# Layer 0 feed-forward: the normalisation and the first scaling of a tile of x move from VectorE to ScalarE, and the measuring of the rows moves within VectorE's tile

## The chip, the cores and the metric

The kernel is one program on one core of a Trainium2 chip. The engines have these names: PE is TensorE (matmuls and transposes, PEld its weight loads), DVE is VectorE, ACT is ScalarE, POOL is GpSimd, and SP issues transfers. The time is device microseconds of the program, from its start to its end; the median of several runs is what is compared. All times in the text are microseconds (us) unless marked ns.

## The reference, cut to what matters

The program computes four layers on x, which is 16 tiles of 128 rows by 256 columns in float32. Each layer is an attention-like part and a feed-forward part, each added to x. The change is in the feed-forward part of layer 0, which works on quantised numbers (a "BitNet" linear layer with a Hadamard transform):

```
x = x + _L0_ffn_ref(_layernorm(x), w_gate, w_up, w_down)

def act_quant(x):                       # per row
    scale = 128 / clip(max(|x|), 1e-5)
    return clip(round(x * scale), -128, 127) / scale
def weight_quant(w):                    # -1, 0, 1 times a mean
    ...
def fwht(x):                            # Walsh-Hadamard transform over 1024 columns
    ...
gate = act_quant(x) @ weight_quant(w_gate).T        # 256 -> 1024
up   = act_quant(x) @ weight_quant(w_up).T          # 256 -> 1024
return act_quant(fwht(silu(gate) * up)) @ weight_quant(w_down).T   # 1024 -> 256
```

`_layernorm` subtracts the row's mean and divides by the root of its variance plus 1e-5.

## The kernel before, in words

The stage is the function `hadamard_ffn`. It handles the 16 tiles t = 0 to 15 as a pipeline written out by hand: each engine has its own program, a function `tile(t, u)` called for every t (u is t modulo 2, the buffer), and the engines meet only at semaphores. An engine does its instructions strictly in the order written; a wait holds everything behind it. `over_long_pipe` calls `tile` for t = 0 and 1, then in a loop for t = 2 to 11, then for the last four written out. `ahead(t, n)` says that tile t + n exists.

What happens to one tile, by engine:

- VectorE, `quantise_x` (L221, then L1348 to L1362): `normalise` writes `xn`, from which the largest magnitude of each row is reduced into `a_max`; `a_rec` is its reciprocal and `deq` the factors for gate and up; then L1358 multiplies `xn` by `a_rec` and adds the constant MAGIC (which rounds), and L1362 subtracts MAGIC again and clips at 127 into the bf16 tile `xq`. Each step is followed by a `drain`, since the next reads what it wrote.
- TensorE, `turn_xq`: two transposes of `xq` into PSUM. ScalarE, `copy_xqT`: copies them to SBUF. TensorE, `gate_up`: eight matmuls of 128x512 in bf16. ScalarE, `silu` (L1428): the gate. VectorE, `gate_times_up` (L1369): gate times up into `prod`.
- GpSimd, `butterflies` (L1336, L1337): six additions and subtractions of 128x512 in float32, between tiles in SBUF, from `prod` by way of `fly` to `mixed`. These are three of the transform's levels. TensorE, `turn_mixed`: eight transposes in two halves, each half copied by ScalarE's `copy_mixedT` (L1434). TensorE, `transform`: 16 matmuls with the Hadamard matrix into `ps_f`.
- VectorE, `scale_h` (L1374 to L1380): largest magnitude of each row of `ps_f`, its reciprocal `b_rec`. ScalarE, `round_h` (L1440). VectorE, `quantise_h` (L1386). TensorE `turn_hq`, ScalarE `copy_hqT`, TensorE `down` (into `ps_y`). VectorE, `add_to_x` (L1390): adds `ps_y` to x, and takes the row statistics for the next stage.

In one call of `tile(t)`, VectorE does quantise_x(t+3), gate_times_up(t+2), scale_h(t), add_to_x(t-1), quantise_h(t). ScalarE does copy_mixedT(t) twice, silu(t+2), copy_hqT(t-1) twice, copy_xqT(t+3), round_h(t). TensorE does turn_mixed(t, first half), the gate of t+2, turn_mixed(t, second half), the up of t+2, transform(t) with turn_hq(t-1) between its halves, turn_xq(t+3), down(t-1). `down(t-1)` also waits for copy_xqT(t+3), since both use the PSUM tile `ps_q`.

Ahead of the first tile GpSimd computes the power -0.5 of all 16 tiles' variances in one instruction (L216, `all_rstd`), then fills a tile of zeros and the one-column tile `magic`. ScalarE waits for `magic` (`const_done`).

Of the kernel before, what the change touches and what calls it, by code (L numbers as in the profile page):

```python
# [8 lines left out]
P = 128  # L9
# [49 lines left out]
        body(t, t % 2)  # L59


def over_ring(eng, body, n, ring, lead=1):

    rest = n % ring or ring
    for j in range(lead * ring):
        body(j, j % ring)
    with eng.Fori(lead, (n - rest) // ring) as i:
        for r in range(ring):
            body(i * ring + r, r)
    for j in range(n - rest, n):  # L70
        body(j, j % ring)
# [1194 lines left out]
def hadamard_ffn(core, name):  # L1266
# [3 lines left out]
    with core.stage() as st:  # L1270
# [3 lines left out]
        def sem(n):  # L1274
            return core.sem(f"{name}_{n}", st)
# [44 lines left out]

        @block.gpsimd
        def _(pool):
            all_rstd(pool, core, rstd_done)
            pool.memset(core.zeros[:, :], 0.0).then_inc(zeroed, 1)
            pool.memset(magic[:, :], MAGIC).then_inc(const_done, 1)

            def butterflies(t, u):

                pool.wait_ge(prod_done, t + 1)
                if after(t, 2):  # L1330
                    pool.wait_ge(mixT_put, t - 1)
                for n, (src, dst) in enumerate(((prod[u], fly), (fly, prod[u]), (prod[u], mixed[u]))):
                    v, o = (m[:, :].rearrange("p (a two c) -> p a two c", two=2, c=P << n) for m in (src, dst))
                    if n:
                        pool.drain()
                    pool.tensor_tensor(o[:, :, 0, :], v[:, :, 0, :], v[:, :, 1, :], ALU.add)  # L1336
                    last = pool.tensor_tensor(o[:, :, 1, :], v[:, :, 0, :], v[:, :, 1, :], ALU.subtract)  # L1337
                last.then_inc(mixed_done, 1)

            over_tiles(pool, butterflies)  # L1340

        @block.vector
        def _(dve):
# [61 lines left out]
            dve.wait_ge(rstd_done, 1)
            quantise_x(0, 0)
            quantise_x(1, 1)
            gate_times_up(0, 0)
            quantise_x(2, 0)
            gate_times_up(1, 1)  # L1410
            over_long_pipe(dve, tile)
            add_to_x(B - 1, 1)
            finish_stats(dve, core)

        @block.scalar
        def _(act):
# [32 lines left out]
            def tile(t, u):  # L1449
# [19 lines left out]
            copy_hqT(B - 1, 1)

# [1314 lines left out]
```

## Time and profile before

| what | us |
|---|---|
| median of 3 runs | 1633.55 (1631.49 to 1633.68) |
| the profiled execution's own time | 1628.51 |
| its span | 1626.7 |
| VectorE busy over the whole span | 1071.2 (66%) |
| TensorE busy | 1352.0 (83%) |
| ScalarE busy | 777.4 (48%) |
| GpSimd busy | 631.9 (39%) |

The stage of the change lies between about 273 us (the last row statistics of the stage before are done) and 456 us in the trace. Busy shares over the whole span say little about it, since the eight stages have different limits; it is read by itself, in the timelines below. Matmuls overlap, so their busy times are not exact, and the names of buffers are without their numbers.

### The profile page before, as it was taken

How to read it: one execution, taken by the hardware profiler on the slowest of the kernel's cores; microseconds unless marked ns; L12 is line 12 of the kernel's file. 1: busy time of each engine (PE TensorE's matmuls, PEld its weight loads, DVE VectorE, ACT ScalarE, POOL GpSimd, SP SyncE). 2: the span in 40 equal slices, each digit the busy share in tenths (PEclk: the TensorE clock that was granted, in tenths of full speed). 3: DMA queues.
4: the chain of work that ended last, by engine and by line, in shares of the span. 5: the costliest groups of instructions: out<-in, count | busy, mean ns of one | idle time of the engine just before them, and what ended most of it. 6: DMA issues, size and time to landing. Idle time of an engine off the chain costs nothing. (4 is left out here: it accounts for less than half of the span.)

```text
span 1626.7 us, 29297 instructions
## 1 busy us (share of the span) xinstructions
PE 1352.0 (83%) x7976; PEld 845.5 (52%) x7992; DVE 1071.2 (66%) x2429; ACT 777.4 (48%) x2322; POOL 631.9 (39%) x649
## 2 busy tenths in 40 slices
PE   3899996566759969799997999978995999978993
PEld 2555553345534434476554666554663666654662
DVE  3898896788748855422664888875334888864224
ACT  2676773344540025432105888842442788833330
POOL 3112420777757523474002112112444665214661
PEclk9999997899979959999997999998998999998997
DMA  4231001400010022397501000141442210411224
GB/s 151 76 83 48 17 15 62 149 0 0 1 52 0 0 84 75 109 303 222 157 1 48 25 28 22 49 159 43 133 128 74 65 49 29 172 55 56 84 84 162
DMA packets 96447, 124.80 MB, mean 77 GB/s; under 512 B 11117, under 2 KB 76464, under 8 KB 96112
## 3 DMA queue, kind: packets, MB, share of 16 engines
q1 hardware_dynamic: 85392, 95.63, 18.5%
q0 software_dynamic: 10608, 28.07, 5.9%
q8 instruction: 36, 0.59, 0.1%
q14 instruction: 43, 0.35, 0.1%
q10 hardware_dynamic: 368, 0.16, 0.0%
HBM read 91.31 MB, written 33.43 MB: 77 GB/s over the span
## 5 line engine op out<-in xcount | busy, mean ns | idle before, releaser
L695 ACT ACTIVATE l0a_prob<-l0a_ps_s,l0a_neg_max 128x128 f32<-128x128 f32 x512 | 137.6, 398 | 67.7 <-DVE l0a_neg_max L553 60.0
L695 ACT ACTIVATE l2a_prob<-l2a_ps_s,l2a_neg_max 128x128 f32<-128x128 f32 x512 | 138.3, 399 | 26.7 <-DVE l2a_neg_max L553 21.7
L1135 ACT ACTIVATE l3a_prob<-l3a_ps_s,l3a_neg_max 128x256 f32<-128x256 f32 x256 | 104.3, 482 | 33.9 <-DVE l3a_neg_max L1050 32.3
L216 POOL TENSOR_TENSOR ln_rstd<-ln_var_eps,minus_half 128x16 f32<-128x16 f32 x7 | 20.5, 2922 | 233.5 <-POOLq L171 207.0
L553 DVE TENSOR_REDUCE l2a_neg_max<-l2a_ps_s 128x4 f32<-128x512 f32 x128 | 85.5, 683 | 19.1 <-PE l2a_ps_s L793 18.1
L501 POOL TENSOR_TENSOR l2a_k_head<-l2a_kT,head_of_row 128x512 f32<-128x512 f32 x32 | 32.9, 1047 | 161.7 <-DMA l2a_kT<-k_rows 161.7
L562 DVE COPY l0a_probT<-l0a_ps_t 128x512 f32<-128x512 f32 x128 | 84.4, 680 | 15.4 <-PE l0a_ps_t L805 15.2
L1050 DVE TENSOR_REDUCE l3a_neg_max<-l3a_ps_s 128x2 f32<-128x512 f32 x128 | 84.0, 679 | 14.2 <-PE l3a_ps_s L1186 13.0
L553 DVE TENSOR_REDUCE l0a_neg_max<-l0a_ps_s 128x4 f32<-128x512 f32 x128 | 85.2, 681 | 10.4 <-PE l0a_ps_s L793 9.6
L1748 PE MATMUL l1a_ps_y<-l1a_kv,l1a_tap 128*128 128x512 f32 x192 | 84.3, 602 | 3.7 <-POOL l1a_kv L1720 3.7
L501 POOL TENSOR_TENSOR l0a_k_head<-l0a_kT,head_of_row 128x512 f32<-128x512 f32 x30 | 30.8, 1047 | 145.6 <-DMA l0a_kT<-k_rows 145.6
L805 PE MATMUL l2a_ps_t<-ident,l2a_prob 128*128 128x128 f32 x512 | 75.6, 281 | 8.0 <-DVE l2a_probT L562 7.0
L805 PEld LDWEIGHTS l2a_ps_t<-ident,l2a_prob 128*128 128x128 f32 x512 | 56.7, 142 | 42.5 <-DVE l2a_probT L562 24.7
L2607 PE MATMUL l3f_ps_g<-l3f_w_gu_all,l3f_xinT 128*128 x156 | 73.5, 593 | 0.0
L805 PE MATMUL l0a_ps_t<-ident,l0a_prob 128*128 128x128 f32 x512 | 69.9, 273 | 1.8 <-DVE l0a_probT L562 1.8
L1198 PE MATMUL l3a_ps_t<-ident,l3a_prob 128*128 128x128 f32 x512 | 69.1, 278 | 2.2 <-ACT l3a_probT L1143 2.0
L1720 POOL TENSOR_TENSOR l1a_kv<-l1a_vT,ctxT_all 128x1024 f32 (+1 forms) x32 | 61.6, 1947 | 18.8 <-PE l1a_ps_y L1748 18.5
L2297 DVE TENSOR_TENSOR l3f_h_sb<-l3f_ps_g,l3f_act_sb 128x256 f32<-128x256 f32 x39 | 16.5, 424 | 77.9 <-ACT l3f_act_sb L2453 77.9
L562 DVE COPY l2a_probT<-l2a_ps_t 128x512 f32<-128x512 f32 x96 | 64.6, 681 | 4.4 <-PE l2a_ps_t L805 4.4
L783 PE MATMUL l0a_ps_s<-l0a_mask,identb 128*128 128x512 bf16 x128 | 49.7, 397 | 21.0 <-ACT l0a_prob L695 21.0
L2071 POOL DMA_INDIRECT l2f_xin<-expert_rows,l2f_tokens x47 | 44.6, 949 | 55.4 <-PE l2f_ps_x L2593 42.1
L1198 PEld LDWEIGHTS l3a_ps_t<-ident,l3a_prob 128*128 128x128 f32 x512 | 56.9, 142 | 17.1 <-ACT l3a_probT L1143 10.9
(477 smaller groups left out, 3532.4 us busy)
## 6 DMA issues: line engine op xcount, KB each, us to landing
l1f_w_gu<-in_l1f_w_gu SPq DMA_DIRECT2D x32, 352.0 KB, 6.8
expert_results<-zeros SPq DMA_DIRECT2D x1, 8320.0 KB, 26.3
l1f_got<-expert_results SPq DMA_DIRECT2D x16, 512.0 KB, 3.9
expert_results<-l2f_y_sb SPq DMA_DIRECT2D x47, 128.0 KB, 1.7
l1f_w_d<-in_l1f_w_d SPq DMA_DIRECT2D x32, 176.0 KB
l2f_w_gu_all<-in_l2f_w_gu SPq DMA_DIRECT2D x1, 4096.0 KB, 15.2
l3f_w_gu_all<-in_l3f_w_gu SPq DMA_DIRECT2D x1, 4096.0 KB, 15.4
l3f_got<-expert_results SPq DMA_DIRECT2D x16, 256.0 KB, 5.0
```

Of the source, the lines that this page charges most:

```text
L501: pool.tensor_tensor(k_head[u][:, c, :, :], kT[u][:, c:c + 1, :].broadcast_to([P, R, P]), core.head_of_row[:, :].unsqueeze(2).broadcast_to ...
L553: dve.tensor_reduce(neg_max[:, j, :], ps_s[j][:, :].rearrange("p (r k) -> p r k", r=R), AX.X, ALU.max, negate=True).then_inc(max_done, 1)
L562: dve.tensor_copy(probT[4 * c + j][:, :], ps_t[j % 2][:, :]).then_inc(t_done_v, 1)
L695: last = act.activation(prob[4 * c + j][:, r * P:r * P + P], ps_s[j][:, r * P:r * P + P], ACT.Exp, bias=neg_max[:, j, r:r + 1])
L783: pe.matmul(ps_s[j][:, :].rearrange("p (r k) -> p r k", r=R), core.identb[:, :], mask[u][:, :].unsqueeze(1).broadcast_to([P, R, P]), start ...
L805: last = pe.transpose(ps_t[j % 2][:, r * P:r * P + P], prob[4 * c + j][:, r * P:r * P + P], core.ident[:, :])
L1050: dve.tensor_reduce(neg_max[:, j, :], ps_s[j][:, :].rearrange("p (r k) -> p r k", r=2), AX.X, ALU.max, negate=True).then_inc(max_done, 1)
L1135: last = act.activation(prob[4 * c + j][:, m * D:m * D + D], ps_s[j][:, m * D:m * D + D], ACT.Exp, bias=neg_max[:, j, m:m + 1])
L1198: last = pe.transpose(ps_t[j % 2][:, k * D + m * P:k * D + m * P + P], prob[4 * c + j][:, m * D + k * P:m * D + k * P + P], core.ident[:, :])
L1720: pool.tensor_tensor(kv[u][:, c, :].rearrange("p (b j i) -> p b j i", b=B, i=N8), i_rows, j_rows, ALU.mult).then_inc(kv_done, 1)
L1748: last = pe.matmul(ps[u][c][:, cols], tap[u][:, (c - m) * P:(c - m) * P + P], kv[u][:, m, cols], start=(m == 0), stop=(m == c))
L2607: last = pe.matmul(ps_g[r % 2][:, 0:2 * FE], xinT[r % 2][:, c, :], w, start=(c == 0), stop=(c == KC - 1))
```

## The change

Five things change, all in `hadamard_ffn`:

1. The normalisation is done by ScalarE (`norm`) as rstd times x plus `shift`, where `shift` = -mean times rstd is one small VectorE instruction for tiles 0 to 2 and one for 3 to 15. `xn` has two buffers. It is done for tile t+5 at the end of ScalarE's tile t.
2. The multiplication by `a_rec` with the addition of MAGIC is done by ScalarE (`round_x`) into a new tile `xr`, for tile t+4, behind `round_h(t)` and ahead of `norm(t+5)`.
3. VectorE's `quantise_x` becomes `measure_x` (reduction, scale, reciprocal, `deq`) for tile t+4 and `clip_x` (the clipping into `xq`) for tile t+3. Both now stand behind `scale_h(t)` and ahead of `add_to_x(t-1)`; before, the whole stood first in the tile.
4. The power is taken in two parts, of 3 and of 13 columns, each with its own signal.
5. The loop now covers t = 2 to 9, and the last six tiles are written out.

TensorE's program is the same as before, and so are GpSimd's six butterflies per tile.

The core of the diff:

```diff
+def rstd_in_parts(pool, core, done):
+    for part in (slice(0, FIRST), slice(FIRST, B)):
+        pool.tensor_tensor(core.rstd[:, part], core.var_eps[:, part], core.minus_half[:, part], ALU.pow).then_inc(done, 1)
...
-            def quantise_x(t, u):
-                dve.drain()
-                normalise(dve, core, xn[:, :], t)
-                dve.drain()
-                dve.tensor_reduce(a_max[:, :], xn[:, :], AX.X, ALU.max, apply_absolute_value=True)
...
-                dve.tensor_scalar(xn[:, :], xn[:, :], a_rec[:, :], MAGIC, ALU.mult, ALU.add)
-                dve.drain()
+            def measure_x(t, u):
+                dve.wait_ge(normed, t + 1)
+                dve.tensor_reduce(a_max[u][:, :], xn[u][:, :], AX.X, ALU.max, apply_absolute_value=True)
+                dve.drain()
+                dve.tensor_scalar(a_max[u][:, :], a_max[u][:, :], 1e-5, 1.0 / 128, ALU.max, ALU.mult)
+                dve.drain()
+                dve.reciprocal(a_rec[:, :], a_max[u][:, :]).then_inc(x_scaled, 1)
+                dve.tensor_scalar(deq[u][:, :], w_mean[:, 0:2], a_max[u][:, :], None, ALU.mult)\
                    .then_inc(deq_done, 1)
+            def clip_x(t):
+                dve.wait_ge(x_rounded, t + 1)
                 if after(t, 1):
                     dve.wait_ge(xqT_put, t)
+                dve.tensor_scalar(xq[:, :], xr[:, :], MAGIC, 127.0, ALU.subtract, ALU.min).then_inc(xq_done, 1)
...
             def tile(t, u):                      # VectorE
-                if ahead(t, 3):
-                    quantise_x(t + 3, 1 - u)
                 if ahead(t, 2):
                     gate_times_up(t + 2, u)
                 scale_h(t, u)
+                if ahead(t, 3):
+                    clip_x(t + 3)
+                if ahead(t, 4):
+                    measure_x(t + 4, u)
                 if after(t, 1):
                     add_to_x(t - 1, 1 - u)
                 quantise_h(t)
...
+            def norm(t, u):                      # ScalarE
+                act.activation(xn[u][:, :], core.xt(t), ACT.Identity, bias=shift[:, bass.ds(t, 1)],
+                               scale=core.rstd[:, bass.ds(t, 1)]).then_inc(normed, 1)
+            def round_x(t, u):
+                act.wait_ge(x_scaled, t + 1)
+                if after(t, 1):
+                    act.wait_ge(xq_done, t)
+                act.activation(xr[:, :], xn[u][:, :], ACT.Identity, bias=magic[:, :], scale=a_rec[:, :])\
+                    .then_inc(x_rounded, 1)
...
                 if ahead(t, 3):
                     copy_xqT(t + 3, 1 - u)
                 round_h(t)
+                if ahead(t, 4):
+                    round_x(t + 4, u)
+                if ahead(t, 5):
+                    norm(t + 5, 1 - u)
```

Ahead of the loop, ScalarE now does norm(0), norm(1), the wait for `magic`, round_x(0), round_x(1), copy_xqT(0), norm(2), copy_xqT(1), silu(0), round_x(2), norm(3), copy_xqT(2), silu(1), round_x(3), norm(4). VectorE does the shifts of three tiles, measure_x(0), clip_x(0), the other shifts, measure_x(1), clip_x(1), gate_times_up(0), measure_x(2), clip_x(2), gate_times_up(1), measure_x(3).

VectorE in one written-out tile, before: the first twelve instructions of it, where `l0f_xn` is the normalised tile, `l0f_prod` the product of gate and up, `ps_f` the transformed product.

```order
L221 TENSOR_SCALAR l0f_xn<-x_rows,ln_mean_var,ln_rstd 128x256
L1348 TENSOR_REDUCE l0f_a_max<-l0f_xn 128x1
L1350 TENSOR_SCALAR l0f_a_max<-l0f_a_max 128x1
L1352 RECIPROCAL l0f_a_rec<-l0f_a_max 128x1
L1355 TENSOR_SCALAR l0f_deq1<-w_mean,l0f_a_max 128x2
L1358 TENSOR_SCALAR l0f_xn<-l0f_xn,l0f_a_rec 128x256
L1362 TENSOR_SCALAR l0f_xq<-l0f_xn 128x256
L1369 SCALAR_TENSOR_TENSOR l0f_prod0<-l0f_ps_u,l0f_deq0,l0f_gate 128x1024
L1374 TENSOR_REDUCE l0f_b_max<-l0f_ps_f 128x1
L1377 TENSOR_SCALAR l0f_b_max<-l0f_b_max 128x1
L1379 TENSOR_SCALAR l0f_b_deq0<-l0f_b_max,w_mean 128x1
L1380 RECIPROCAL l0f_b_rec<-l0f_b_max 128x1
```

The same engine after, from gate_times_up on (L1390 is now that line, L1383 clips, L1371 to L1376 measure, L1411 adds to x).

```order
L1390 SCALAR_TENSOR_TENSOR l0f_prod1<-l0f_ps_u,l0f_deq1,l0f_gate 128x1024
L1395 TENSOR_REDUCE l0f_b_max<-l0f_ps_f 128x1
L1398 TENSOR_SCALAR l0f_b_max<-l0f_b_max 128x1
L1400 TENSOR_SCALAR l0f_b_deq1<-l0f_b_max,w_mean 128x1
L1401 RECIPROCAL l0f_b_rec<-l0f_b_max 128x1
L1383 TENSOR_SCALAR l0f_xq<-l0f_xr 128x256
L1371 TENSOR_REDUCE l0f_a_max1<-l0f_xn1 128x1
L1373 TENSOR_SCALAR l0f_a_max1<-l0f_a_max1 128x1
L1375 RECIPROCAL l0f_a_rec<-l0f_a_max1 128x1
L1376 TENSOR_SCALAR l0f_deq1<-w_mean,l0f_a_max1 128x2
L1411 SCALAR_TENSOR_TENSOR x_rows<-l0f_ps_q,l0f_b_deq0,x_rows 128x256
L205 BN_STATS ln_partial<-x_rows 128x6
```

Five instructions stood between the start of the tile and the writing of `xq`; now `xq` is written behind the four instructions of `scale_h`, and the two wide operations on `xn` are gone from this engine.

ScalarE in one written-out tile before, from the copies of `mixedT` to those of the next tile (`l0f_rounded` is round_h).

```order
L1434 ACTIVATE l0f_mixedT<-l0f_ps_t 128x512 x2
L1428 ACTIVATE l0f_gate<-l0f_ps_g,l0f_deq0 128x1024
L1447 ACTIVATE l0f_hqT<-l0f_ps_q 128x512 x2
L1421 ACTIVATE l0f_xqT1<-l0f_ps_q 128x256
L1440 ACTIVATE l0f_rounded<-l0f_ps_f,l0f_magic,l0f_b_rec 128x1024
L1434 ACTIVATE l0f_mixedT<-l0f_ps_t 128x512 x2
```

The same after: L1475 copies `mixedT`, L1469 is the gate, L1488 copies `hqT`, L1462 copies `xqT`, L1481 is round_h, L1455 round_x, L1448 norm.

```order
L1475 ACTIVATE l0f_mixedT<-l0f_ps_t 128x512 x2
L1469 ACTIVATE l0f_gate<-l0f_ps_g,l0f_deq0 128x1024
L1488 ACTIVATE l0f_hqT<-l0f_ps_q 128x512 x2
L1462 ACTIVATE l0f_xqT1<-l0f_ps_q 128x256
L1481 ACTIVATE l0f_rounded<-l0f_ps_f,l0f_magic,l0f_b_rec 128x1024
L1455 ACTIVATE l0f_xr<-l0f_xn0,l0f_magic,l0f_a_rec 128x256
L1448 ACTIVATE l0f_xn1<-x_rows,l0f_shift,ln_rstd 128x256
L1475 ACTIVATE l0f_mixedT<-l0f_ps_t 128x512 x2
```

Two instructions now stand between round_h and the next tile's first copy of `mixedT`; the copy of `xqT` stands ahead of round_h in both.

## Rows read from the trace of the kernel before

**Rows 1.** Busy time in a stretch: engine busy us (instructions), clock, DMA share, GB/s

```profile
301.96:423.09 121.13, 81.65 (x580) 60.27 (x592) 104.02 (x179) 58.44 (x84) 97.47 (x74) 0.94 0.00 0
```

**Rows 2.** Timeline, VectorE, one tile (start us, duration us, what [idle before])

```profile
342.54 0.29 DVE L1362 TENSOR_SCALAR l0f_xq<-l0f_xn 128x256 bf16<-128x256 f32 x1
342.74 1.28 DVE L1369 SCALAR_TENSOR_TENSOR l0f_prod<-l0f_ps_u,l0f_deq,l0f_gate 128x1024 f32<-128x1024 f32 x1
343.94 1.21 DVE L1374 TENSOR_REDUCE l0f_b_max<-l0f_ps_f 128x1 f32<-128x1024 f32 x1
...
345.62 0.16 DVE L1380 RECIPROCAL l0f_b_rec<-l0f_b_max 128x1 f32<-128x1 f32 x1
...
347.15 1.48 DVE L1386 TENSOR_SCALAR l0f_hq<-l0f_rounded 128x1024 bf16<-128x1024 f32 x1 [0.28 <-ACT l0f_rounded L1440]
348.97 0.94 DVE L221 TENSOR_SCALAR l0f_xn<-x_rows,ln_mean_var,ln_rstd 128x256 f32 x1 [0.34 <-issue]
349.98 0.42 DVE L1348 TENSOR_REDUCE l0f_a_max<-l0f_xn 128x1 f32<-128x256 f32 x1
...
350.71 0.16 DVE L1352 RECIPROCAL l0f_a_rec<-l0f_a_max 128x1 f32<-128x1 f32 x1
...
351.29 1.25 DVE L1358 TENSOR_SCALAR l0f_xn<-l0f_xn,l0f_a_rec 128x256 f32<-128x256 f32 x1
```

**Rows 3.** Timeline, GpSimd, the same tile

```profile
344.18 1.26 POOL L1336 TENSOR_TENSOR l0f_fly<-l0f_prod 128x512 f32<-128x512 f32 x1 [1.87 <-DVE l0f_prod L1369]
345.40 1.26 POOL L1337 TENSOR_TENSOR l0f_fly<-l0f_prod 128x512 f32<-128x512 f32 x1
...
351.12 1.26 POOL L1337 TENSOR_TENSOR l0f_mixed<-l0f_prod 128x512 f32<-128x512 f32 x1
```

**Rows 4.** Timeline, ScalarE, the same tile

```profile
343.28 0.38 ACT L1421 ACTIVATE l0f_xqT<-l0f_ps_q 128x256 bf16<-128x256 bf16 x1 [1.23 <-PE l0f_ps_q L1480]
345.82 1.20 ACT L1440 ACTIVATE l0f_rounded<-l0f_ps_f,l0f_magic,l0f_b_rec 128x1024 f32<-128x1024 f32 x1 [2.15 <-DVE l0f_b_rec L1380]
346.92 0.59 ACT L1434 ACTIVATE l0f_mixedT<-l0f_ps_t 128x512 f32<-128x512 f32 x1
348.25 0.60 ACT L1434 ACTIVATE l0f_mixedT<-l0f_ps_t 128x512 f32<-128x512 f32 x1 [0.75 <-PE l0f_ps_t L1502]
348.75 1.11 ACT L1428 ACTIVATE l0f_gate<-l0f_ps_g,l0f_deq 128x1024 f32<-128x1024 f32 x1
```

**Rows 5.** Timeline, VectorE, the last tiles

```profile
430.20 1.28 DVE L1369 SCALAR_TENSOR_TENSOR l0f_prod<-l0f_ps_u,l0f_deq,l0f_gate 128x1024 f32<-128x1024 f32 x1 [1.30 <-ACT l0f_gate L1428]
...
438.89 1.23 DVE L1374 TENSOR_REDUCE l0f_b_max<-l0f_ps_f 128x1 f32<-128x1024 f32 x1 [3.22 <-PE l0f_ps_f L1511]
...
446.20 1.22 DVE L1374 TENSOR_REDUCE l0f_b_max<-l0f_ps_f 128x1 f32<-128x1024 f32 x1 [3.52 <-PE l0f_ps_f L1511]
```

**Rows 6.** Timeline, ScalarE, the last tiles

```profile
429.06 1.11 ACT L1428 ACTIVATE l0f_gate<-l0f_ps_g,l0f_deq 128x1024 f32<-128x1024 f32 x1
...
443.18 0.60 ACT L1434 ACTIVATE l0f_mixedT<-l0f_ps_t 128x512 f32<-128x512 f32 x1 [0.75 <-PE l0f_ps_t L1502]
```

**Rows 7.** Timeline, VectorE, the first tiles

```profile
284.90 1.28 DVE L1369 SCALAR_TENSOR_TENSOR l0f_prod<-l0f_ps_u,l0f_deq,l0f_gate 128x1024 f32<-128x1024 f32 x1 [3.89 <-PE l0f_ps_u L1491]
...
290.43 1.19 DVE L1362 TENSOR_SCALAR l0f_xq<-l0f_xn 128x256 bf16<-128x256 f32 x1
295.31 1.28 DVE L1369 SCALAR_TENSOR_TENSOR l0f_prod<-l0f_ps_u,l0f_deq,l0f_gate 128x1024 f32<-128x1024 f32 x1 [3.69 <-PE l0f_ps_u L1491]
```

**Rows 8.** Groups by line, GpSimd: the power on three columns

```profile
L1002 POOL TENSOR_TENSOR ln_rstd<-ln_var_eps,minus_half 128x3 f32<-128x3 f32 x1 | 0.9, 888 | 0.0
```

**Rows 9.** Timeline, GpSimd, the stage's first instructions

```profile
273.24 2.92 POOL L216 TENSOR_TENSOR ln_rstd<-ln_var_eps,minus_half 128x16 f32<-128x16 f32 x1 [35.92 <-POOLq L171]
...
276.37 0.09 POOL L1325 MEMSET l0f_magic<- 128x1 f32 x1
```

**Rows 10.** Timeline, ScalarE, the next stage's first normalisations

```profile
460.25 1.09 ACT L1663 ACTIVATE l1a_xn<-x_rows,l1a_shift,ln_rstd 128x256 f32<-128x256 f32 x2 [8.10 <-DVE l1a_shift L1627]
```

More of the change, by code:

```diff
@@ L59, in over_long_pipe, with over_x_pipe @@
         body(t, t % 2)
+def over_x_pipe(eng, body):
+    body(0, 0)
+    body(1, 1)
+    with eng.Fori(1, B // 2 - 3) as i:
+        body(i * 2, 0)
+        body(i * 2 + 1, 1)
+    for t in range(B - 6, B):
+        body(t, t % 2)
 def over_ring(eng, body, n, ring, lead=1):
@@ L1281, in hadamard_ffn @@
         magic = sb("magic", [P, 1])
-        xn = sb("xn", [P, D])
+        xn = [sb(f"xn{u}", [P, D]) for u in range(2)]
+        xr = sb("xr", [P, D])
+        shift = sb("shift", [P, B])
         xq = sb("xq", [P, D], BF16)
         xqT = [sb(f"xqT{u}", [P, KC, P], BF16) for u in range(2)]
-        a_max, a_rec = sb("a_max", [P, 1]), sb("a_rec", [P, 1])
+        a_max, a_rec = [sb(f"a_max{u}", [P, 1]) for u in range(2)], sb("a_rec", [P, 1])
         deq = [sb(f"deq{u}", [P, 2]) for u in range(2)]
@@ L1405, in _ @@
             dve.wait_ge(rstd_done, 1)
-            quantise_x(0, 0)
-            quantise_x(1, 1)
+            shifts(0, FIRST)
+            measure_x(0, 0)
+            clip_x(0)
+            dve.wait_ge(rstd_done, 2)
+            shifts(FIRST, B)
+            measure_x(1, 1)
+            clip_x(1)
             gate_times_up(0, 0)
-            quantise_x(2, 0)
+            measure_x(2, 0)
+            clip_x(2)
             gate_times_up(1, 1)
-            over_long_pipe(dve, tile)
+            measure_x(3, 1)
+            over_x_pipe(dve, tile)
             add_to_x(B - 1, 1)
@@ L1459, in tile @@
                 round_h(t)
+                if ahead(t, 4):
+                    round_x(t + 4, u)
+                if ahead(t, 5):
+                    norm(t + 5, 1 - u)
+            act.wait_ge(shift_done, 1)
+            norm(0, 0)
+            norm(1, 1)
             act.wait_ge(const_done, 1)
+            round_x(0, 0)
+            round_x(1, 1)
             copy_xqT(0, 0)
+            norm(2, 0)
             copy_xqT(1, 1)
             silu(0, 0)
+            round_x(2, 0)
+            act.wait_ge(shift_done, 2)
+            norm(3, 1)
             copy_xqT(2, 0)
             silu(1, 1)
-            over_long_pipe(act, tile)
+            round_x(3, 1)
+            norm(4, 0)
+            over_x_pipe(act, tile)
             copy_hqT(B - 1, 0)
```

16 lines of the change are left out of this document (7 added, 9 removed).

## The prediction

> **What bounds the kernel now.** I first read the busy times of the stage, then the timelines of the four engines over one tile, one engine at a time, and last the first and the last tiles. Call G(t) the start of gate_times_up of tile t and S(t) the start of scale_h of tile t. From G(2) at 301.96 to G(14) at 423.09, the ends of the window that I asked for, there are 12 tiles in 121.13 us, 10.09 each, with VectorE busy 104.02 and GpSimd 97.47 of it, ScalarE only 58.44 [rows 1]. So VectorE looks like the bound. The timelines say something narrower. L1358, a 256-column operation, takes 1.25 us, and it ends at 352.54, which is 0.16 after GpSimd's last butterfly (351.12 + 1.26 = 352.38) [rows 2, 3]. L1362, an operation of the same width and kind, takes 0.29 when GpSimd is idle and 1.19 when it is not [rows 2, 7]. I read this as: VectorE's single-source operations between SBUF tiles wait for the end of the butterfly in progress. No semaphore shows it, only the duration. So before, one turn of the cycle is G to GpSimd's start 1.44 (344.18 - 342.74), six butterflies to 352.38 (8.20), 0.16, then the clipping and the next G, about 0.4: 10.05 in all. The cycle runs through both engines.
>
> The reader should see a second chain beneath it. In the last tiles, where nothing is left to quantise, S to S is 7.31 (446.20 - 438.89) [rows 5]. It goes over round_h, the two copies of mixedT and the transform.
>
> **What the change takes away.** Per tile, L221 (0.94) and L1358 (1.25) leave VectorE, with some drains [rows 2]. That takes GpSimd's last butterfly out of the cycle: clipping alone is left of the wide operations ahead of the next copy. If VectorE were all that counts, 2.2 us a tile times 12 would be 26 us. It will not be, because the order of the steps makes a new chain.
>
> **The new chain.** clip_x(t+3) now stands behind scale_h(t) on VectorE. turn_xq(t+3) waits for it, copy_xqT(t+3) waits for that, and on ScalarE round_h(t), round_x(t+4), norm(t+5) and then the next tile's copies of mixedT are queued behind copy_xqT(t+3). Before, xq was written ahead of scale_h, so copy_xqT was long done (343.28) when round_h began (345.82) [rows 4]. The steps, from the end of clip_x:
>
> - to copy_xqT: 0.45 (xq ends 342.83, copy starts 343.28) [rows 2, 4]
> - to round_h: 0.28. The copy lasts 0.38, and ScalarE starts its next instruction some 0.10 before the last one ends (346.92 against 347.02) [rows 4]
> - to round_x: 1.10 (346.92 - 345.82) [rows 4]
> - to norm and from norm to the first copy of mixedT: 0.50 each; two such instructions take 1.09 together and one 0.59 [rows 4, 10]
> - to the second copy of mixedT: 1.33 [rows 4]
> - to silu: 0.50 [rows 4]; from silu to the next G: 1.14 (430.20 - 429.06) [rows 5, 6]
>
> Sum: 0.45 + 0.28 + 1.10 + 0.50 + 0.50 + 1.33 + 0.50 + 1.14 = 5.80 from the end of clip_x to the next G.
>
> When does clip_x end? By the transform, S follows the second copy by 3.02 (446.20 - 443.18) [rows 5, 6], G by 0.50 + 1.14 = 1.64, so S = G + 1.38. scale_h ends 1.84 after S (345.78 - 343.94) [rows 2], so clip_x begins at G + 3.25 or a little later. GpSimd is then in its second butterfly, which ends at G + 3.92 (345.40 + 1.26 - 342.74) [rows 3]. Adding 0.16, clip_x ends at G + 4.08 instead of G + 3.6. The period is 4.08 + 5.80 = 9.88 us against 10.09. Almost all that VectorE gives up is taken by the new chain.
>
> All else has room: six butterflies need 8.2 of 9.88; measure_x needs 0.89 to its reciprocal (350.87 - 349.98) [rows 2] and has 1.1 under round_h; quantise_h, 1.48 at most, falls after add_to_x, before the next silu is done. If that cover were gone, quantise_h would delay the next G one for one. TensorE's program is unchanged. The down matmuls and the first transposes of the next tile shift later with copy_xqT and fit beside round_h to norm; I give them nothing. The bound for norm's addresses, computed from a register in the loop, is 0 from one side (hidden behind round_x) and 0.34 from the other, VectorE's idle issue time ahead of L221 [rows 2]. I take 0, since ScalarE has no drain in front.
>
> At this place a rule bears on the sum. By the trace, 0.29 becomes 1.19 beside a butterfly. The Trainium skill (SBUF — State Buffer, Who interferes with whom) says that whichever of GpSimd and a two-port VectorE operation issues first gets the shared ports for the whole instruction and the other fully blocks. By that rule, the trace agrees, the period is 9.88; if clip_x were not held it would be 9.4 (second rival below).
>
> **The start.** The power of 3 columns takes 0.89 [rows 8], of 16 columns 2.92 [rows 9]; a straight line through both gives 2.45 for 13, so both parts end 0.42 later than the one did. ScalarE can normalise early, but round_x(0) waits for `magic`, ready at 276.46 before [rows 9], now 276.9. So the split hardly shows. Bounds of that term: -0.42 to +2.0 (2.92 - 0.89) if nothing waited for `magic`. From 276.9: round_x(0) 0.64, clip 0.29, the second shifts 0.25, measure_x(1) 0.89, round_x(1) 0.64, clip 0.34: 279.95. The wait from there to G(0) was 3.89 [rows 7], so G(0) = 283.9, 1.0 earlier than 284.90. Then clip_x(2): measure at G + 1.2, 0.89, round_x 0.64, then held until G + 4.08 = 288.0; before, xq(2) ended at 291.62 [rows 7]. G(1) follows 3.69 later: 291.7, 3.6 earlier. This is the best part of the change: three stalls beside the butterflies become one. Then measure_x(3) to 293.8, round_x(3) and norm(4) 0.5 each, copies 1.33, 0.50, 1.14: G(2) = 297.8, 4.2 earlier than 301.96.
>
> **The sum.** Of the 12 tiles to G(14), the first two find GpSimd still behind with tiles 1 and 2, and the end of a butterfly falls closer behind scale_h: about 9.4 each. The other ten at 9.88; the last lacks a norm (-0.5): 18.8 + 98.8 - 0.5 = 117.1 against 121.13, a gain of 4.0. G(15) - G(14) was 7.11 (430.20 - 423.09) [rows 1, 5], because no xq was left to make. Now clip_x(15) still falls there: 4.08 + 5.80 - 1.00 = 8.88, a loss of 1.8. After that both are alike, 7.31 a tile. 4.2 + 4.0 - 1.8 = 6.4 us. Against the profiled execution's own time, 1628.51 (span 1626.7, 1.8 outside): 1622.1. That execution lies 5.0 under the median, so I take the same 6.4 off the median: 1633.55 - 6.4 = 1627.1.
>
> **The rivals.**
>
> A page of the Trainium skill speaks against the change (Perfetto Trace Analysis, Optimizing Scalar/DVE Operations): what VectorE does in a performance mode it does faster, and giving it to ScalarE may make sense only when VectorE is saturated. The first rival is what that would mean here.
>
> 1. About the same: the steady part gives nothing. ScalarE's two instructions lengthen the chain where VectorE was not the limit. If norm's address work is exposed, 0.34 in 8 looped tiles is 2.7; small waits of 0.1 a tile on TensorE make 1.2 more. 6.4 - 3.9 = 2.5: 1631.0. For it: every step sits on one chain. Against: before, ScalarE's looped instructions show no such gap.
>
> 2. Faster than forecast: clip_x is not held. It then ends at S + 2.18, and from S to S the chain is 2.18 + 0.45 + 0.28 + 1.10 + 1.00 + 1.33 + 3.02 = 9.36. Twelve tiles: 111.8, gain 9.3; the start gains 5.2 (one hold of 1.0 less); G(15) costs 1.3. Total 13.2: 1620.3. Against it: the 1.19 beside a butterfly [rows 7]. For it: clip_x could fall in the short gap that GpSimd's drain leaves between its second and third butterfly.
>
> 3. Slower: clip_x misses that gap. It starts at G + 3.25, the gap is at G + 3.92. If it comes 0.7 us later (a longer transform, a late signal), it waits for the third butterfly, G + 5.34, and ends 1.42 later each tile. Over 11 tiles that is 15.6; 6.4 - 15.6 = -9.2: 1642.7. The point where it decides is a delay of 0.7. For it: S hangs on TensorE's transform, and each tile repeats the phase of the last. Against: 0.7 is more than any spread in the rows.
>
> That the change doesn't do what it says (the rows' work stays on VectorE's path through clip_x) is contained in rival 1.
>
> **Chances.** Forecast 0.60, rival 1 0.17, rival 2 0.13, rival 3 0.10. A measurement of this kernel tells about 0.2%, 3.3 us, from no change. Faster by more: the forecast but for its low edge (0.57) and rival 2 (0.13): 0.70. Within: 0.03 + 0.15 = 0.18 with most of rival 1. Slower: rival 3 and the rest of rival 1, 0.12. The range takes rival 2 and rival 1 whole and leaves rival 3 out: 1619.5 to 1635.
>
> **What would show it.** In the profile after: clip_x at about 1 us with its end 0.16 behind GpSimd's second butterfly; ScalarE idle ahead of copy_xqT for some 2.5 us, waiting for TensorE's transposes, and none ahead of round_h; G to G 9.9; VectorE idle more than 1 us before gate_times_up with silu as releaser; G(2) near 297.8; G(14) to G(15) near 8.9. Clip_x at 0.3, or ending behind the third butterfly, would make the forecast wrong, as would G to G set by GpSimd's six butterflies.

## The result: slower by 0.7%, and the profile after

The changed kernel takes 1645.67 us (median of four runs; three lie between 1643.93 and 1646.73, and the fourth, disturbed, took 2364.31 at a granted clock of 0.646 and is left out of the ratio; without it the median is 1644.62) against 1632.95 for the kernel before: a ratio of 1.0067, 95% interval 1.0038 to 1.0097. I had forecast 1627.1, in a range of 1619.5 to 1635. A second measurement, on another chip, gave 1.0072 (1.0039 to 1.0105).

From the stage's first power instruction to that of the next stage, the profiled execution before took 457.10 - 273.24 = 183.9 us; after, 474.98 - 275.48 = 199.5. These 15.6 us are the whole difference of the two spans (1626.7 and 1642.1), so the other stages are not involved. (The medians differ by 12.7 only; the profiled execution before was 4.4 below its median.)

The table gives the starts of gate_times_up, G(t), read from VectorE's timeline, relative to the stage's first power instruction.

| | before | forecast | after |
|---|---|---|---|
| G(2) | 28.7 | 24.6 | 24.4 |
| G(2) to G(14) | 121.1 | 117.1 | 136.0 |
| G(14) to G(15) | 7.1 | 8.9 | 10.8 |

The start is as forecast; the steady part is 19 us longer than forecast. First its busy times, in the order PE, PEld, DVE, ACT, POOL, then the granted clock of TensorE:

```profile
299.88:435.84 135.96, 97.61 (x586) 70.07 (x585) 83.22 (x154) 68.23 (x105) 94.12 (x75) 0.80 0.04 12
```

The clock is 0.80, against 0.94 before [rows 1]. VectorE is busy 83 of 136 us, and no engine is full. Now one tile, engine by engine. VectorE, where L1390 is gate_times_up, L1395 and L1401 are scale_h, L1383 is clip_x:

```profile
344.12 1.28 DVE L1390 SCALAR_TENSOR_TENSOR l0f_prod<-l0f_ps_u,l0f_deq,l0f_gate 128x1024 f32<-128x1024 f32 x1 [1.51 <-ACT l0f_gate L1469]
345.42 1.22 DVE L1395 TENSOR_REDUCE l0f_b_max<-l0f_ps_f 128x1 f32<-128x1024 f32 x1
...
347.08 0.15 DVE L1401 RECIPROCAL l0f_b_rec<-l0f_b_max 128x1 f32<-128x1 f32 x1
347.16 1.04 DVE L1383 TENSOR_SCALAR l0f_xq<-l0f_xr 128x256 bf16<-128x256 f32 x1
...
356.33 1.28 DVE L1390 SCALAR_TENSOR_TENSOR l0f_prod<-l0f_ps_u,l0f_deq,l0f_gate 128x1024 f32<-128x1024 f32 x1 [2.47 <-ACT l0f_gate L1469]
```

GpSimd in the same tile, its first two butterflies:

```profile
345.57 1.26 POOL L1357 TENSOR_TENSOR l0f_fly<-l0f_prod 128x512 f32<-128x512 f32 x1 [3.50 <-DVE l0f_prod L1390]
346.79 1.26 POOL L1358 TENSOR_TENSOR l0f_fly<-l0f_prod 128x512 f32<-128x512 f32 x1
```

clip_x begins at G + 3.04 and lasts 1.04 instead of 0.29. It ends at 348.20, which is G + 4.08 and 0.15 behind the second butterfly (348.05). That is exactly as forecast. ScalarE then (L1462 copy_xqT, L1481 round_h, L1455 round_x, L1448 norm, L1475 the copies of mixedT, L1469 silu):

```profile
348.76 0.38 ACT L1462 ACTIVATE l0f_xqT<-l0f_ps_q 128x256 bf16<-128x256 bf16 x1 [2.52 <-PE l0f_ps_q L1536]
349.04 1.20 ACT L1481 ACTIVATE l0f_rounded<-l0f_ps_f,l0f_magic,l0f_b_rec 128x1024 f32<-128x1024 f32 x1
350.13 0.60 ACT L1455 ACTIVATE l0f_xr<-l0f_xn,l0f_magic,l0f_a_rec 128x256 f32<-128x256 f32 x1
350.62 0.59 ACT L1448 ACTIVATE l0f_xn<-x_rows,l0f_shift,ln_rstd 128x256 f32 x1
352.04 0.60 ACT L1475 ACTIVATE l0f_mixedT<-l0f_ps_t 128x512 f32<-128x512 f32 x1 [0.83 <-PE l0f_ps_t L1558]
354.60 0.60 ACT L1475 ACTIVATE l0f_mixedT<-l0f_ps_t 128x512 f32<-128x512 f32 x1 [1.96 <-PE l0f_ps_t L1558]
355.10 1.11 ACT L1469 ACTIVATE l0f_gate<-l0f_ps_g,l0f_deq 128x1024 f32<-128x1024 f32 x1
```

Up to norm each step is as in the prediction: 0.28, 1.09, 0.49. Then the two copies of mixedT wait for TensorE's transposes (L1558), 0.83 and 1.96 us. From the first copy to the second it takes 2.56 instead of 1.33 [rows 4]. TensorE shows why (L1536 turn_xq, L1590 down, L1558 turn_mixed, L1547 gate and up):

```profile
348.33 0.39 PE L1536 MATMUL l0f_ps_q<-identb,l0f_xq 128*128 128x128 bf16 x2 [2.73 <-DVE l0f_xq L1383]
349.29 1.87 PE L1590 MATMUL l0f_ps_q<-w_int,l0f_hqT 128*128 128x256 bf16 x8 [0.57 <-ACT l0f_xqT L1462]
350.95 1.06 PE L1558 MATMUL l0f_ps_t<-ident,l0f_mixed 128*128 128x128 f32 x4
351.80 1.91 PE L1547 MATMUL l0f_ps_g<-w_int,l0f_xqT 128*128 128x512 bf16 x4
353.51 1.06 PE L1558 MATMUL l0f_ps_t<-ident,l0f_mixed 128*128 128x128 f32 x4
```

It stands idle 2.73 us until clip_x is done. After that the eight matmuls of down take 1.87, four transposes 1.06 and the gate 1.91. In the kernel before, in a tile with a granted clock of 1.00 (342.74 to 352.82), the same work is faster (L1534 down, L1502 turn_mixed, L1491 up, which is as large as the gate):

```profile
343.81 1.03 PE L1534 MATMUL l0f_ps_q<-w_int,l0f_hqT 128*128 128x256 bf16 x8 [0.57 <-ACT l0f_xqT L1421]
344.68 0.60 PE L1502 MATMUL l0f_ps_t<-ident,l0f_mixed 128*128 128x128 f32 x4
348.05 1.03 PE L1491 MATMUL l0f_ps_u<-w_int,l0f_xqT 128*128 128x512 bf16 x4
```

The granted clock of the change, in two stretches of this tile and the next (columns as above):

```profile
348.20:355.00 6.80, 6.11 (x24) 3.97 (x25) 3.48 (x7) 3.45 (x6) 4.97 (x4) 0.50 0.00 0
361.70:365.20 3.50, 3.50 (x15) 2.26 (x14) 1.73 (x3) 2.13 (x4) 3.36 (x3) 0.52 0.00 0
```

0.50 is the lower of the chip's two levels, 1.2 GHz, and 1.00 the upper, 2.4 GHz. So the mean of 0.80 is made of both. Read in steps of 1 us, the clock falls in eleven of the twelve tiles from G(2) to G(14), for about 3.5 us in some and about 6.8 us in others; from G(4) on the tiles of the short falls take 10.8 to 11.3 us and those of the long ones 12.1 to 12.2. The tile shown is a long one; the next, from 356.33, takes 11.18. In the one tile without a fall of its own, from G(3), the transform still ran at the low clock of the fall before it.

The sum of this tile: the wait ahead of the first copy is 0.92 more than the forecast's, the second copy comes 1.23 later, and 0.11 and 0.09 are lost around turn_xq and silu. 9.88 + 2.35 = 12.2, which is 356.33 - 344.12. The waits from 320 to 436 us (who waited for whom, total us, times, longest) give the same picture:

```profile
POOL l0f_fly L1357 <- DVE l0f_prod L1390: 36.8, 10, 4.5
...
PE l0f_ps_q L1536 <- DVE l0f_xq L1383: 26.4, 10, 2.7
...
DVE l0f_prod L1390 <- ACT l0f_gate L1469: 23.2, 11, 2.7
ACT l0f_mixedT L1475 <- PE l0f_ps_t L1558: 22.8, 20, 2.0
```

TensorE waits 2.64 us a tile for clip_x; ScalarE waits for the transposes; VectorE waits for silu; GpSimd waits for VectorE, and its second butterfly holds clip_x. None of them is the bound by itself; it is one ring through all four.

At the start of the stage, GpSimd's timeline after (the two parts of the power are merged in one row):

```profile
275.48 3.27 POOL L234 TENSOR_TENSOR ln_rstd<-ln_var_eps,minus_half 128x3 f32<-128x3 f32 x2 [34.98 <-POOLq L183]
...
278.95 0.09 POOL L1346 MEMSET l0f_magic<- 128x1 f32 x1
```

And ScalarE's first round_x:

```profile
279.08 0.60 ACT L1455 ACTIVATE l0f_xr<-l0f_xn,l0f_magic,l0f_a_rec 128x256 f32<-128x256 f32 x1 [1.40 <-POOL l0f_magic L1346]
```

Both parts take 3.27 together against 2.92 [rows 9]. norm(0) and norm(1) are done early, and then round_x(0) waits for `magic`, which comes behind both parts, as forecast.

### The profile page after: what moved, and what is told of

Same layout as the page of the kernel before. It is cut to its first block and busy times, and to the rows that moved or that the text cites. A ratio compares the mean times of both kernels' runs of the same rounds, so it can differ in the third digit from the quotient of the medians.

```text
span 1642.1 us, 29264 instructions
## 1 busy us (share of the span) xinstructions
PE 1373.7 (84%) x7991; PEld 858.0 (52%) x7992; DVE 1043.2 (64%) x2399; ACT 793.1 (48%) x2354; POOL 628.5 (38%) x650
## 5 line engine op out<-in xcount | busy, mean ns | idle before, releaser
L1068 DVE TENSOR_REDUCE l3a_neg_max<-l3a_ps_s 128x2 f32<-128x512 f32 x128 | 84.0, 680 | 13.9 <-PE l3a_ps_s L1204 12.7
L1776 POOL TENSOR_TENSOR l1a_kv<-l1a_vT,ctxT_all 128x1024 f32 (+1 forms) x32 | 61.6, 1947 | 19.2 <-PE l1a_ps_y L1804 18.8
```

The source lines that it names most:

```text
L1068: dve.tensor_reduce(neg_max[:, j, :], ps_s[j][:, :].rearrange("p (r k) -> p r k", r=2), AX.X, ALU.max, negate=True).then_inc(max_done, 1)
L1776: pool.tensor_tensor(kv[u][:, c, :].rearrange("p (b j i) -> p b j i", b=B, i=N8), i_rows, j_rows, ALU.mult).then_inc(kv_done, 1)
```

## The experiments

The theory after the result: the placing of clip_x behind scale_h makes TensorE wait, the wait takes its clock, and a slow TensorE stands in the chain. Its rivals: the chain is longer than I summed whatever the clock; ScalarE's two added instructions are the cost. Nine kernels ran. In the table, "a tile" is G(2) to G(12), divided by ten, from the traces; "stage" is from its first power instruction to that of the next stage; the ratio is to the kernel before, timed beside it on the same chip.

| run | a tile, us | stage, us | ratio (95% interval) |
|---|---|---|---|
| before | 10.10 | 183.9 | 1 |
| the change | 11.28 | 199.5 | 1.0067 (1.0038 to 1.0097) |
| e1_warm | 9.86 | 180.1 | 0.9932 (0.9905 to 0.9959) |
| e2_clip_first | 8.52 | 160.2 | 0.9842 (0.9804 to 0.9880) |
| e3_before_clip_late | 11.88 | 209.2 | 1.0136 (1.0097 to 1.0175) |
| e4_clip_after_measure | 10.59 | 187.1 | 1.0025 (0.9998 to 1.0053) |
| e5_one_power | 8.26 | 159.0 | 0.9824 (0.9789 to 0.9860) |
| e6_magic_first | 8.27 | 158.8 | 0.9863 (0.9825 to 0.9901) |
| e7_before_warm | 10.11 | 184.2 | 1.0000 (0.9960 to 1.0040) |
| e8_after_again | 11.28 | 200.1 | 1.0072 (1.0039 to 1.0105) |
| e9_late_clip_warm | 11.34 | 204.2 | 1.0136 (1.0059 to 1.0213) |

The kernels e1 to e3 ran on one chip, e4 to e6 on a second and e7 to e9 on a third. On the second the kernel before took 1654.0 us against 1633.45 and 1629.6 on the others, so times are compared only by ratio. The ratio is not exactly the quotient of the two medians (for e1 0.9932 and 0.9946). The whole program also varies outside the stage; the stage's length is the sharper number.

**e1_warm.** TensorE fills its wait.

```diff
                 if ahead(t, 3):
+                    keep_busy(pe, core, ps_t, 8)
                     turn_xq(t + 3, 1 - u)
```

> The changed kernel, and TensorE does 8 extra matmuls of 128x512 in bf16 into the empty transposing tile just ahead of the transposes of xq, where it waited 2.6 us a tile for clip_x. Nothing else is touched, and their results are not used. Theory 1 (the clock): the wait lets TensorE's granted clock fall (0.80 in the steady part against 0.94 before), its matmuls between copy_xqT and silu then take up to twice as long and stand in the chain; with the gap filled the clock is back above 0.9, a tile takes 9.9 us instead of 11.3, and the time is 1645.7 - 12 x 1.4 = about 1629. Rival (the chain itself is longer than I summed, clock or not): the period stays at 11.3 and the time at 1645 or up to 1650, since the fillers only add work.

1624.63 us (before 1633.45). The busy times of the steady part, columns as above:

```profile
299.50:417.39 117.89, 97.43 (x683) 64.65 (x682) 83.83 (x154) 67.23 (x105) 97.56 (x74) 1.00 0.04 13
```

TensorE in one tile (L199 are the filling matmuls):

```profile
340.07 1.89 PE L199 MATMUL l0f_ps_t<-identb 128*128 128x512 bf16 x8
342.97 0.28 PE L1536 MATMUL l0f_ps_q<-identb,l0f_xq 128*128 128x128 bf16 x2 [1.01 <-DVE l0f_xq L1383]
343.82 1.03 PE L1590 MATMUL l0f_ps_q<-w_int,l0f_hqT 128*128 128x256 bf16 x8 [0.56 <-ACT l0f_xqT L1462]
344.69 0.60 PE L1558 MATMUL l0f_ps_t<-ident,l0f_mixed 128*128 128x128 f32 x4
345.12 1.03 PE L1547 MATMUL l0f_ps_g<-w_int,l0f_xqT 128*128 128x512 bf16 x4
```

ScalarE in the same tile (copy_xqT and the two copies of mixedT):

```profile
343.29 0.38 ACT L1462 ACTIVATE l0f_xqT<-l0f_ps_q 128x256 bf16<-128x256 bf16 x1 [2.43 <-PE l0f_ps_q L1536]
...
345.64 0.59 ACT L1475 ACTIVATE l0f_mixedT<-l0f_ps_t 128x512 f32<-128x512 f32 x1
346.98 0.60 ACT L1475 ACTIVATE l0f_mixedT<-l0f_ps_t 128x512 f32<-128x512 f32 x1 [0.75 <-PE l0f_ps_t L1558]
```

The clock is 1.00. down takes 1.03, the transposes 0.60, the gate 1.03, and the second copy follows the first by 1.34. G(2) to G(14) is 417.39 - 299.50 = 117.9 us, against 136.0 in the change and 117.1 in the forecast. So adding work made this part 18 us shorter. With the clock held, the forecast's chain is right to 0.7%. The rival of a longer chain is out. (The ratio says 11 us faster than before, the stage only 3.8; the rest is outside the stage and not explained.)

**e2_clip_first.** clip_x first in VectorE's tile.

```diff
+                if ahead(t, 3):
+                    clip_x(t + 3)
                 if ahead(t, 2):
                     gate_times_up(t + 2, u)
                 scale_h(t, u)
-                if ahead(t, 3):
-                    clip_x(t + 3)
```

> The changed kernel with one call moved: clip_x(t+3) stands first in VectorE's tile, ahead of gate_times_up and scale_h, as xq's writing did before the change. ScalarE keeps the normalisation and the scaling. Theory 1 (the loss comes from clip_x behind scale_h, which puts turn_xq and copy_xqT ahead of round_h, and lets TensorE idle and lose its clock): round_h starts 1.9 after scale_h again, the chain from S to S is 1.9 + 1.1 + 1.0 + 1.33 + 3.02 = 8.35, GpSimd's butterflies (8.2) nearly bind, the clock is back at 0.95, 8.4 to 8.6 us a tile, and the time is about 1633 - 4 - 12 x 1.5 = 1611 (1608 to 1616). Rival (ScalarE's two added instructions or their late signals are the cost): 10 us a tile or more, 1630 or above.

1605.27 us (before 1633.45): 1.6% faster than the kernel before and better than both kernels. VectorE in one tile (the start of scale_h and its reciprocal):

```profile
343.20 1.23 DVE L1395 TENSOR_REDUCE l0f_b_max<-l0f_ps_f 128x1 f32<-128x1024 f32 x1
...
344.86 0.15 DVE L1401 RECIPROCAL l0f_b_rec<-l0f_b_max 128x1 f32<-128x1 f32 x1
```

GpSimd, the last butterfly of one tile and the first of the next:

```profile
342.03 1.28 POOL L1358 TENSOR_TENSOR l0f_mixed<-l0f_prod 128x512 f32<-128x512 f32 x1
343.28 1.26 POOL L1357 TENSOR_TENSOR l0f_fly<-l0f_prod 128x512 f32<-128x512 f32 x1
```

ScalarE, copy_xqT and round_h:

```profile
344.40 0.38 ACT L1462 ACTIVATE l0f_xqT<-l0f_ps_q 128x256 bf16<-128x256 bf16 x1 [0.38 <-PE l0f_ps_q L1536]
345.05 1.21 ACT L1481 ACTIVATE l0f_rounded<-l0f_ps_f,l0f_magic,l0f_b_rec 128x1024 f32<-128x1024 f32 x1 [0.27 <-DVE l0f_b_rec L1401]
```

TensorE, turn_xq:

```profile
344.08 0.29 PE L1536 MATMUL l0f_ps_q<-identb,l0f_xq 128*128 128x128 bf16 x2 [0.69 <-ACT l0f_hqT L1488]
```

round_h starts 1.85 after scale_h's start, as before the change, and not 3.6 (349.04 - 345.42). GpSimd starts the next tile's butterflies (343.28) while the last one of the tile before is just ending (342.03 + 1.28 = 343.31), with no idle time. From here its six butterflies and the chain by way of round_h, both about 8.3 us, are the bound; which of the two is not shown. The time is below the 1608 to 1616 that I expected. ScalarE's two added instructions are on that chain, and yet the tile is 1.6 us shorter than before the change, so they are not the cause. The looped norm starts 0.49 after round_x (346.65 and 346.16), so the 0.34 of address work of the first rival is hidden.

**e3_before_clip_late.** The kernel before, with only the placing of the clipping changed.

```diff
                 if ahead(t, 3):
                     quantise_x(t + 3, 1 - u)      # now without its last instruction
                 if ahead(t, 2):
                     gate_times_up(t + 2, u)
                 scale_h(t, u)
+                if ahead(t, 3):
+                    clip_x(t + 3)
```

> The kernel before, with only the placing of the clipping changed: VectorE still normalises and scales at the start of its tile, but writes xq behind scale_h as the changed kernel does. Theory 1 (the placing is the cause): TensorE waits for xq, copy_xqT and round_h come late, 11.5 us a tile or more and a clock below 0.9, the time 1650 (1642 to 1660). Rival (moving work to ScalarE is the cause, the placing is harmless because xq is only needed a tile later): 10.1 us a tile, 1633.

1656.76 us, slower than the kernel before by 1.36%. TensorE in one tile (L1487 turn_xq, L1541 down):

```profile
351.22 0.28 PE L1487 MATMUL l0f_ps_q<-identb,l0f_xq 128*128 128x128 bf16 x2 [2.73 <-DVE l0f_xq L1364]
352.07 1.86 PE L1541 MATMUL l0f_ps_q<-w_int,l0f_hqT 128*128 128x256 bf16 x8 [0.56 <-ACT l0f_xqT L1428]
353.73 1.06 PE L1509 MATMUL l0f_ps_t<-ident,l0f_mixed 128*128 128x128 f32 x4
```

The same wait of 2.73 us and the same slow matmuls (1.86 for down) appear with nothing moved to ScalarE, at a granted clock of 0.78 from G(2) to G(14). In the kernel before, the placing alone brings a loss. How much of it is the clock, e9 tells.

**e4_clip_after_measure.** In the kernel of e1, with 14 filling matmuls.

```diff
-                if ahead(t, 3):
-                    clip_x(t + 3)
                 if ahead(t, 4):
+                    dve.wait_ge(x_rounded, t + 4)
                     measure_x(t + 4, u)
+                if ahead(t, 3):
+                    clip_x(t + 3)
```

> The run with the filling matmuls (1624.6), with clip_x(t+3) moved behind measure_x(t+4), still ahead of add_to_x, and 14 filling matmuls in place of 8 so that TensorE's longer wait stays filled. It tests the point of decision of the third rival: clip_x now comes to its turn at about G + 4.6, past the end of GpSimd's second butterfly (G + 3.92). Theory (a wide VectorE operation waits for the end of the butterfly in progress): it is held until the third one ends, G + 5.34 + 0.16 = 5.50; the period is 5.50 + 5.80 = 11.3 and the time 1624.6 + 12 x 1.4 = 1641. Rival (it runs as soon as its turn comes, and its 1 us has another reason): it ends at G + 4.9, a tile takes 10.7, 1634.

The ratio, 1.0025, is 0.9% above that of e1, about 15 us; but the stage is only 7.0 longer and a tile 0.73, so most of the ratio's step is not from the stage. By the trace, neither expectation is met as it stands. The tiles go between about 10.1 and 11.3. L1383 is clip_x. VectorE in a tile of the short sort, G at 342.09:

```profile
346.06 0.28 DVE L1383 TENSOR_SCALAR l0f_xq<-l0f_xr 128x256 bf16<-128x256 f32 x1
```

GpSimd in that tile, its second and third butterflies:

```profile
344.75 1.27 POOL L1358 TENSOR_TENSOR l0f_fly<-l0f_prod 128x512 f32<-128x512 f32 x1
346.17 1.30 POOL L1357 TENSOR_TENSOR l0f_prod<-l0f_fly 128x512 f32<-128x512 f32 x1
```

VectorE in the next tile, of the long sort, G at 352.21:

```profile
356.25 1.37 DVE L1383 TENSOR_SCALAR l0f_xq<-l0f_xr 128x256 bf16<-128x256 f32 x1
```

GpSimd in that one, its third butterfly:

```profile
356.21 1.26 POOL L1357 TENSOR_TENSOR l0f_prod<-l0f_fly 128x512 f32<-128x512 f32 x1
```

In the first tile clip_x starts at G + 3.97 in the gap between the second butterfly's end (346.02) and the third's start (346.17), and takes 0.28. In the second tile it starts 0.04 after the third butterfly has begun (356.25 and 356.21), takes 1.37 and ends 0.15 behind it (357.62 and 357.47). That is the hold that the theory said, and the price of missing the gap, 1.2 us a tile, is near the 1.42 of the third rival. What I had wrong was the turn, G + 4.0 and not 4.6: measure_x takes only 0.9 us in front of it, so many of the tiles just catch the gap.

**e5_one_power** and **e6_magic_first.** In the kernel of e2, the power undivided; and `magic` filled ahead of the two parts.

```diff
-            rstd_in_parts(pool, core, rstd_done)                  # e5
+            all_rstd(pool, core, rstd_done)
```

```diff
+            pool.memset(magic[:, :], MAGIC).then_inc(const_done, 1)   # e6
             rstd_in_parts(pool, core, rstd_done)
             pool.memset(core.zeros[:, :], 0.0).then_inc(zeroed, 1)
-            pool.memset(magic[:, :], MAGIC).then_inc(const_done, 1)
```

> The run with clip_x first (1605.3), with the power undivided: one instruction for 16 tiles, one signal, one instruction for the shifts. Theory (the split buys nothing, since round_x(0) waits for magic, which comes behind both parts): magic is ready 0.35 earlier, the first product of gate and up 0.5 earlier, and the time is 1604.8, no different within what can be measured. Rival (the early normalisation of three tiles pays): 1 to 2 us slower, 1606 to 1607.

> The run with clip_x first (1605.3), with the filling of magic ahead of the power on GpSimd. Theory (the split only pays when nothing waits behind both parts): round_x(0) starts when a_rec(0) is there, some 1.3 us earlier, but round_x(1) still needs the second part; the first product comes about 1 us earlier, and the time is 1604.3. Rival (nothing at the start is on the path, since GpSimd's butterflies set the pace later): 1605.3.

Ratios 0.9824 and 0.9863, against 0.9842 for e2: the intervals overlap, and no difference between the three is shown. From the first power instruction to G(0) it takes 10.4 us in e2, 11.2 with one power, and 9.5 with `magic` first. So the split wins 0.8 there, where I had expected it to lose 0.5: undivided, round_x(0) waits for `a_rec` and starts 4.8 after the power, against 3.6. With `magic` first it wins 0.8 more. At the end of the stage nothing is left of it (160.2, 159.0, 158.8). Part of that is chance: one tile of e2 had a low clock and took 10.35.

**e7_before_warm, e8_after_again, e9_late_clip_warm.** On one chip: the kernel before with the eight fillers of e1, the change again without any edit, and e3 with the fillers. The edit in e7 and e9:

```diff
                 if ahead(t, 3):
+                    keep_busy(pe, core, ps_t, 8)
                     turn_xq(t + 3, 1 - u)
```

> A control: the kernel before, with the same 8 filling matmuls on TensorE ahead of the transposes of xq. Theory (the fillers help the changed kernel only because its chain runs over a TensorE at half clock; before, the clock was 0.94 and the cycle ran over GpSimd and VectorE): no change, 10.1 us a tile, within 0.2% of the kernel before. Rival (the fillers speed up the stage by some other way, or the clock cost the kernel before as well): 3 us or more faster.

> The changed kernel again, unedited, on the same chip as the two runs beside it: 1.0067 of the kernel before, as first measured (1.0038 to 1.0097), by every theory.

> The kernel before with only the clipping placed behind scale_h (12.0 us a tile, 1.0136 of before), and with the 8 filling matmuls. Theory (the placing costs twice: a longer chain at any clock, and the clock): the chain at full clock is VectorE's, clip_x to G + 4.1, add_to_x, quantise_h, normalise and scale each held by a butterfly, 11.4 us a tile; so 12 x 0.6 = 7 us faster than without fillers, 1.009 of before. Rival (all of the loss is the clock): 10.1 us a tile, 1.000.

e7 is the control: in the kernel before, the fillers bring the clock from 0.94 to 0.99 and change nothing else (10.11 a tile, ratio 1.0000). The cycle there does not pass over TensorE. e8 repeats the loss. For e9 the timing decides nothing, since its interval is wide. Its trace shows 11.34 us a tile against 11.88 in e3, at a clock of 0.89 on average (it still falls in some tiles). So in the kernel before, the late clipping costs 1.2 us a tile with the clock mostly held, and 0.5 more with it lost; that rival is out too. VectorE around one G of it (L221 normalises, L1371 is gate_times_up, L1364 clips):

```profile
343.91 0.91 DVE L221 TENSOR_SCALAR l0f_xn<-x_rows,ln_mean_var,ln_rstd 128x256 f32 x1 [0.37 <-issue]
...
346.32 1.28 DVE L1371 SCALAR_TENSOR_TENSOR l0f_prod<-l0f_ps_u,l0f_deq,l0f_gate 128x1024 f32<-128x1024 f32 x1
...
349.62 0.78 DVE L1364 TENSOR_SCALAR l0f_xq<-l0f_xn 128x256 bf16<-128x256 f32 x1 [0.22 <-issue]
```

clip_x ends at G + 4.08 here too (350.40), and in front of G the normalisation (0.91 instead of 0.4) is again held by a butterfly.

## Why the prediction was wrong

Point by point, by its own steps:

- **What bounds the kernel before: right.** The cycle over GpSimd and VectorE is confirmed by e7: filling TensorE does not touch it.
- **clip_x held by the butterfly: right.** From G(4) to G(14) in the change it ends at G + 3.99 to 4.08, for a forecast of 4.08, and e4 shows both sides of the edge 0.15 us apart.
- **The chain from clip_x to the next G, 5.80: right at full clock.** In e1 it is 5.86 in the tile shown (342.84 to 348.70), and from G(4) to G(12) a tile takes 9.89; the forecast was 9.88.
- **"TensorE's program is unchanged. The down matmuls and the first transposes of the next tile shift later with copy_xqT and fit beside round_h to norm; I give them nothing": this is the step that failed.** I took TensorE's durations from a stretch with a granted clock of 0.94. The new chain makes it stand idle 2.6 us a tile in one piece, just ahead of that work; its clock falls to half in eleven of twelve tiles (0.80 on average), and in the tile shown down, the transposes and the gate take 1.87, 1.06 and 1.91. They then no longer fit beside ScalarE's instructions. The missing term is 2.3 us in the tile above. Over G(2) to G(14) it is 136.0 - 117.9 = 18.1 us, read from e1. Without it the forecast would have stood: e1 gives 0.9932, and the forecast was 0.9961 of the median. That this is even better than forecast is luck: e1's stage is 3.8 us shorter than before and not 6.4, and the rest comes from outside the stage.
- **The start: right in its sum, half right in its reason.** G(2) comes 24.4 after the first power instruction, for a forecast of 24.6. round_x(0) waits for `magic`, as said, but the split was not worthless: without it (e5) G(0) comes 0.8 later.
- **G(14) to G(15): 10.8, forecast 8.9.** In e1 it is 9.4, so most of it is the same missing term once more.
- **"After that both are alike": not quite.** From G(15) to the next stage it takes 28.3, before 26.9. TensorE's granted clock is 0.81 there, before 0.90; e1, whose fillers stop ahead of this part, has 28.2 and 0.82. That this 1.4 us is the clock again is likely, but no run isolates it.
- **The whole stage.** The forecast was 183.9 - 6.4 = 177.5, the change took 199.5. The 22.0 between them are -0.2 up to G(2), 18.9 to G(14), 1.9 to G(15) and 1.4 after it.
- **The third rival named the right sign by the wrong mechanism.** Its 1642.7 is near the measured time, but I let it depend on clip_x missing the gap in each tile. It misses it once in the change, in the tile from G(3) (it ends at 314.97, G + 5.59), and there because the slow transform had put scale_h 1.4 us later. That its price was near is luck. I had looked for slower cases only in the order of instructions, not in their durations.

The warning was in the kernel before. In its first tiles TensorE waits long for xq, and its clock there is 0.51 (273.24 to 284.90 us) and 0.67 (284.90 to 295.31), while the steady part, whose waits for xq are 1.6 us a tile (19.2 in 12), has 0.94. The Trainium skill (TensorE: Matmul & The Clock Gate, HAM oscillation — how this bites in real kernels) describes the same pattern with waits for transfers: matmuls in bursts with a wait between them fall back to the half rate in every round. The trace agrees on the pattern, in eleven of twelve tiles and with waits for another engine, but its waits of 2.64 us are shorter than those of the page's example, so the page alone would not have foretold it; e1 settles what it cost.

## What to carry to other kernels

When a change makes TensorE wait in one longer piece, its durations may no longer be taken from rows at full clock: sum the chain once with the matmuls at each level, and see whether they still fit beside what they ran beside. When work is divided between two engines, what decides is where the small instruction stands that a third one waits for: here one call of 0.3 us, moved by a few lines, turned a loss of 0.7% into a gain of 1.6%. And where filling idle time with useless matmuls makes a kernel faster, as here in e1 and not in e7, its clock is what it lacks.

## What the runs showed of the hardware that I had not expected

- TensorE fell to 1.2 GHz in nearly every tile in a kernel that keeps it busy 72% of the time by its records: 97.61 us of 135.96, of which a part is itself the slowness (1.87 for 1.03). Ahead of the falls it had waited 2.2 to 2.7 us; one wait of 2.75, ended at 315.02, brought none, and why is open. With the wait partly filled (1.01 left in the tile shown) the clock was 1.00.
- The edge of the hold by GpSimd is sharp. Starting 0.11 ahead of the next butterfly, a 256-column clipping took 0.28; starting 0.04 after one had begun, 1.37. And it is regular: in the change, all fourteen clip_x that began during a butterfly ended 0.14 to 0.16 after the end of one.
- In e2 the two engines still hold each other up (in the tile shown clip_x takes 1.37, and a butterfly 1.78 beside quantise_h), and the tile is shorter all the same, because clip_x has nobody waiting for it there.
